# Scores of two heads at the head of every second step, and a new order of a head's products

## The reference, cut to what matters

```python
x = x + tanh(g_xattn[0]) * cross_attention(layernorm(x), ctx)        # 16 heads of 128
x = x + tanh(g_ffn[0])   * mixture_of_lora(layernorm(x))             # 2 of 8 experts of rank 16
x = x + tanh(g_xattn[1]) * sigmoid_attention(layernorm(x), ctx)
x = x + tanh(g_ffn[1])   * chosen_expert(layernorm(x))               # 1 of 8 experts of rank 64
```

## Time and profile before

| what | value |
|---|---|
| median of 3 executions | 1353.68 us (1353.68 to 1355.13) |
| the profiled execution | 1354.27 us |
| its span, first to last instruction | 1351.7 us |
| mean granted TensorE clock | 0.999 |
| TensorE matmuls busy | 1327.7 us, 98% |
| TensorE weight loads busy | 1156.7 us, 86% |
| VectorE, ScalarE busy | 766.8 and 765.9 us, 57% each |
| GpSimd busy | 65.1 us, 5% |
| DMA | 108.5 MB, 24.3% of the 16 engines' span |

### The profile page before, as it was taken

One profiled execution on the slowest core, in us unless ns is written; L12 is line 12 of the kernel. 1 busy time (PEld: TensorE's weight loads), 2 busy tenths in 40 slices (PEclk: granted clock), 3 DMA queues, 4 the chain that ended last, 5 costly groups with the idle time before them and its releaser, 6 DMA issues.

```text
span 1351.7 us, 26645 instructions
## 1 busy us (share of the span) xinstructions
PE 1327.7 (98%) x10389; PEld 1156.7 (86%) x10389; DVE 766.8 (57%) x2317; ACT 765.9 (57%) x2092; POOL 65.1 (5%) x112
## 2 busy tenths in 40 slices
PE   8899999999999999999999999999999999999998
PEld 8788888988898888988889888998889888888777
DVE  6654555646565565655656465564656555554575
ACT  4375567566465574756556564555646556456522
POOL 0000000010000000010000100001000000001010
PEclk9999999999999999999999999999999999999999
DMA  8312532123121321223212131122302112122100
GB/s 299 115 63 79 141 107 67 64 84 110 43 79 63 94 94 48 65 93 91 82 48 86 64 118 64 48 79 95 109 34 79 63 63 95 50 77 66 60 1 32
DMA packets 51451, 108.47 MB, mean 80 GB/s; under 512 B 8224, under 2 KB 32000, under 8 KB 50688
## 3 DMA queue, kind: packets, MB, share of 16 engines
q1 hardware_dynamic: 51328, 106.77, 24.3%
HBM read 89.98 MB, written 16.78 MB: 79 GB/s over the span
## 4 chain that ended last, share of the span: by engine, by line
PE 87%; DVE 9%; ACT 2%; issue 1%; DMA 0%; SPq 0%; DVEq 0%
PE bank L114 57%; PE bank L1043 8%; PE bank L1053 5%; PE bank L1014 3%; PE bank L1032 3%; PE bank L1153 2%; PE bank L1165 2%; PE bank L983 2%; PE bank L1004 1%; PE bank L1195 1%; PE bank L1107 1%; ACT xn L780 1%; DVE logit L1542 1%; DVE ao_lo L1533 1%; DVE rstd L80 1%
## 5 line engine op out<-in xcount | busy, mean ns | idle before, releaser
L114 PE MATMUL bank<-sv,ct_hi 128*128 128x256 f32 x1024 | 195.8, 290 | 0.0
L114 PE MATMUL bank<-so,ao_hi 128*128 128x256 f32 x1016 | 187.1, 283 | 0.3 <-DVE ao_lo L1533 0.3
L1533 DVE SCALAR_TENSOR_TENSOR ao_lo<-bank,vecs,ao_hi 128x512 fp32r<-128x512 f32 x127 | 95.3, 751 | 159.8 <-ACT ao_hi L749 158.9
L755 ACT ACTIVATE expo<-logit,least 128x64 f32<-128x64 f32 x512 | 171.6, 337 | 20.6 <-DVE least L1544 20.5
L749 ACT ACTIVATE ao_hi<-bank,vecs 128x512 fp32r<-128x512 f32 x127 | 87.0, 685 | 155.0 <-PE bank L1043 154.5
L114 PEld LDWEIGHTS bank<-so,ao_hi 128*128 128x128 f32 x1016 | 161.6, 188 | 8.5 <-issue 0.5
L114 PEld LDWEIGHTS bank<-sv,ct_hi 128*128 128x128 f32 x1024 | 156.7, 189 | 0.1
L1542 DVE TENSOR_TENSOR logit<-bank,rr 128x256 f32<-128x256 f32 x128 | 54.4, 425 | 162.5 <-PE bank L1053 161.9
L774 ACT ACTIVATE q_sb<-bank,qbias,qscale 128x512 f32<-128x512 f32 x128 | 99.3, 776 | 80.1 <-PE bank L114 79.6
L114 PE MATMUL bank<-sv,ct_lo 128*128 128x256 f32 x512 | 143.3, 280 | 0.0
L114 PE MATMUL bank<-so,ao_lo 128*128 128x256 f32 x508 | 141.9, 279 | 0.0
(11 more groups left out here) (239 smaller groups left out, 2666.4 us busy)
## 6 DMA issues: line engine op xcount, KB each, us to landing
sv<-v_scratch SPq DMA_DIRECT2D x56, 512.0 KB, 3.4
so<-o_scratch SPq DMA_DIRECT2D x56, 512.0 KB, 3.3
xin<-in_x_dram SPq DMA_DIRECT2D x8, 512.0 KB, 5.0
cin<-in_ctx_dram SPq DMA_DIRECT2D x32, 128.0 KB, 4.8
xres<-in_x_dram SPq DMA_DIRECT2D x8, 512.0 KB, 4.6
c_scratch<-cs SPq DMA_DIRECT2D x8, 512.0 KB, 5.0
v_scratch<-sv SPq DMA_DIRECT2D x8, 512.0 KB, 3.1
o_scratch<-so SPq DMA_DIRECT2D x8, 512.0 KB, 2.6
```

The costliest lines, as they stand in the source:

```text
L114: last = pe.matmul(out, lhs[a], rhs[b], start=start and n == 0, stop=stop and n == 2, **kw)
L755: last = act.activation(expo[:, t, :], logit[:, t, :], ACT.Exp, scale=-1.0, bias=least[:, t:t + 1], accum_out=rsum[:, t:t + 1])
L1533: dve.scalar_tensor_tensor(out=lo[:, :], in0=attention_bank(g, h)[:, :], scalar=vecs[:, v:v + 1], in1=hi[:, :].bitcast(F32), op0=ALU.add, ...
```

## The change

TensorE's step becomes: in steps of even h first scores(h-2) and scores(h-1), one behind the other; then k(h), share a, attend(h-3), share b, v(h), share c, q(h), prob_transpose(h-2), share d, output(h-3), share e. ScalarE begins a step with exps(h-2) and k's eviction; q's eviction stands ahead of its copy of the probabilities in odd steps and behind it in even ones. VectorE makes the logits of both heads at the head of an even step, waiting for the second's scores; probabilities and attn_lo come ahead of share a in even steps and behind it in odd ones; its copy of the probabilities comes behind shares b and c (before: ahead of them). The low part of the next group's context is made in step 15 of the group before. Bank 4 holds the scores of two heads; q_sb, logit, least and rsum are doubled, the exponentials overwrite the logits, and gt lies in th. Outputs lag by three heads, not four. The pipeline's emptying has a new order, and in it the last heads use banks and buffers of their own; the late weights' places move by one point. Cut to its core:

```diff
-TURN_LAG, ATT_LAG, OUT_LAG = 2, 3, 4
+TURN_LAG, ATT_LAG, OUT_LAG = 2, 3, 3
-    q_sb = sb("q_sb", [P, GT])
-    logit = sb("logit", [P, NT, SEQ])
-    expo = sb("expo", [P, NT, SEQ])
+    q_sb = sb("q_sb", [P, 2, GT])
+    logit = sb("logit", [P, 2, NT, SEQ])
-    gt = sb("gt", [E1, GT])
+    gt = th[0:E1, 0, :, :].rearrange("p c d -> p (c d)")
-    LATE_AT = {(14, "c"): 0, (14, "d"): 1, (14, "e"): 2, (15, "a"): 3, (15, "b"): 4, (15, "c"): 5, (15, "d"): 6}
+    LATE_AT = {(14, "c"): 0, (14, "d"): 1, (14, "e"): 2, (15, "b"): 3, (15, "c"): 4, (15, "d"): 5, (15, "e"): 6}
...
@@ ScalarE
         def step(b, h):
             main = live(b, h)
+            final = main and h == H - 1 and not is_body(b, NG - 1)
+            if live(b, h - TURN_LAG):
+                exps(b, h - TURN_LAG)
+            if main:
+                project(b, h, 0)
             share(b, h, "a")
             if live(b, h - ATT_LAG):
                 attn_hi(b, h - ATT_LAG)
+            share(b, h, "b")
             if main:
-                project(b, h, 0)
-            share(b, h, "b")
+                project(b, h, 1)
+                if final:
+                    split_context(b + 1)
+            share(b, h, "c")
+            soon = main and (h % 2 == 1 or (b, h) == (LAST, H - 2))
+            if soon:
+                project(b, h, 2)
             if live(b, h - TURN_LAG):
                 prob_copy(b, h - TURN_LAG)
-            share(b, h, "c")
-            if live(b, h - 1):
-                exps(b, h - 1)
-            if main:
-                project(b, h, 1)
-                if h == H - 1 and not is_body(b, NG - 1):
-                    split_context(b + 1)
+            if main and not soon:
+                project(b, h, 2)
+            if final:
+                split_tokens(b + 1)
             share(b, h, "d")
-            if main:
-                project(b, h, 2)
-                if h == H - 1 and not is_body(b, NG - 1):
-                    split_tokens(b + 1)
             share(b, h, "e")
...
@@ TensorE
         def scores(g, h):
             pe.wait_ge(pj_read.sem, pj_read.count(g, 3 * h + 2))
-            l_ready.wait(pe, g, h - 1)
+            l_ready.wait(pe, g, h - 1 if (g, h) == (LAST, H - 1) else h - 1 - h % 2)
...
         def step(b, h):
             main = live(b, h)
+            if (b, h) == (0, 2):
+                gr_read.wait(pe, 0, 2 * NT - 1)
+            if h % 2 == 0 and live(b, h - 2):
+                scores(b, h - 2)
+                scores(b, h - 1)
+            if (b, h) == (LAST, H - 1):
+                scores(b, h - 1)
+            if main and (b, h) != (0, 0):
+                project(b, h, 0)
+            share(b, h, "a")
+            if live(b, h - ATT_LAG):
+                attend(b, h - ATT_LAG)
+            share(b, h, "b")
+            if main:
+                values(b, h)
+            share(b, h, "c")
+            if (b, h) == (0, 1):
+                norms(-1)
+            if main:
+                project(b, h, 2)
+            if live(b, h - TURN_LAG):
+                prob_transpose(b, h - TURN_LAG)
+            share(b, h, "d")
             if live(b, h - OUT_LAG):
                 output(b, h - OUT_LAG)
-            if live(b, h - ATT_LAG):
-                attend(b, h - ATT_LAG)
-            share(b, h, "a")
-            if main and (b, h) != (0, 0):
-                project(b, h, 0)
-            share(b, h, "b")
-            if (b, h) == (0, 1):
-                norms(-1)
-                gr_read.wait(pe, 0, 2 * NT - 1)
-            if live(b, h - 1):
-                scores(b, h - 1)
-            if live(b, h - TURN_LAG):
-                prob_transpose(b, h - TURN_LAG)
-            share(b, h, "c")
-            if main:
-                values(b, h)
-            share(b, h, "d")
-            if main:
-                project(b, h, 2)
+            if (b, h) == (LAST, H - 1):
+                scores(b, h)
             share(b, h, "e")
...
@@ VectorE
         def step(b, h):
-            if h == 0 and not is_body(b, 0) and live(b, 0):
-                split(b, 0)
+            main = live(b, h)
+            if h % 2 == 0 and live(b, h - 2):
+                logits(b, h - 2)
+                logits(b, h - 1)
+            if (b, h) == (LAST, H - 1):
+                logits(b, h - 1)
+            if main and h == 0 and not is_body(b, 0):
+                split(b, 1)
+            if h % 2:
+                share(b, h, "a")
             if live(b, h - TURN_LAG):
                 probabilities(b, h - TURN_LAG)
-            if h == 0 and not is_body(b, 0) and live(b, 0):
-                split(b, 1)
-            share(b, h, "a")
             if live(b, h - ATT_LAG):
                 attn_lo(b, h - ATT_LAG)
-            if is_body(b, 0) and h == 1:
+            if (b, h) == (0, 1):
                 score_factors(0)
-            if live(b, h - 1):
-                logits(b, h - 1)
+            if h % 2 == 0:
+                share(b, h, "a")
+            share(b, h, "b")
+            share(b, h, "c")
             if live(b, h - TURN_LAG):
                 prob_copy(b, h - TURN_LAG)
-            share(b, h, "b")
-            share(b, h, "c")
+            if main and h == H - 1 and not is_body(b, NG - 1):
+                split(b + 1, 0)
             share(b, h, "d")
             share(b, h, "e")
...
@@ TensorE, emptying the pipeline
-        scores(LAST, H - 1)
-        gate_logits(NEXT)
-        output(LAST, H - 4)
+        turned_gates(NEXT)
+        prob_transpose(LAST, H - 2)
         attend(LAST, H - 3)
-        prob_transpose(LAST, H - 2)
+        prob_transpose(LAST, H - 1)
         attend(LAST, H - 2)
-        prob_transpose(LAST, H - 1)
         output(LAST, H - 3)
         attend(LAST, H - 1)
+        gate_logits(NEXT)
         output(LAST, H - 2)
         output(LAST, H - 1)
...
@@ VectorE, end()
             scales_at_once(LAST, 0, xres)
+            expert_scale(NEXT)
             for t in range(3):
                 chosen_expert(NEXT, t)
```

More of the change, by code:

```diff
@@ L175, in layers @@
     nqk_t = sb("nqk_t", [P, 2 * NT])
-    least = sb("least", [P, NT])
-    rsum = sb("rsum", [P, NT])
+    least = sb("least", [P, 2, NT])
+    rsum = sb("rsum", [P, 2, NT])
     rinv = sb("rinv", [P, NT])
@@ L464, in layers @@
                  "lg": (H + 1, "d"), "choice": (H + 1, "e"), "ex1": (H + 2, "a"), "scale": (H + 2, "a")}
[L465 removed]
+    LAST_CHOICE_AT = {"xn3": (14, "d"), ("xt3", 0): (15, "b"), ("xt3", 1): (15, "c")}
     def choice_at(b, h, p, name):
@@ L487, in attention_bank @@
     def attention_bank(g, h):
-        return pj_ps[0] if (g, h) == (LAST, H - 2) else pv_ps
+        return {(LAST, H - 2): pj_ps[0], (LAST, H - 1): at_ps}.get((g, h), pv_ps)
     def attention_parts(g, h):
-        return [v["k"][:, 0, 0:GT] for v in (w_hi, w_lo)] if (g, h) == (LAST, H - 2) else [ao_hi, ao_lo]
+        own = g == LAST and h >= H - 2
+        return [v["k"][:, h - (H - 2), 0:GT] for v in (w_hi, w_lo)] if own else [ao_hi, ao_lo]
     def turned_probs(g, h, t):
@@ L754, in exps @@
             for t in range(NT):
-                last = act.activation(expo[:, t, :], logit[:, t, :], ACT.Exp, scale=-1.0, bias=least[:, t:t + 1],
-                                      accum_out=rsum[:, t:t + 1])
+                last = act.activation(logit[:, h % 2, t, :], logit[:, h % 2, t, :], ACT.Exp, scale=-1.0, bias=least[:, h % 2, t:t + 1],
+                                      accum_out=rsum[:, h % 2, t:t + 1])
             last.then_inc(e_ready.sem, 1)
@@ L760, in prob_copy @@
             act.wait_ge(pt_full.sem, pt_full.count(g, h))
+            if g == LAST and h >= H - 2:
+                act.wait_ge(pv_full.sem, pv_full.count(g, h - 1))
             act.activation(pt_part(0), turned_probs(g, h, 0), ACT.Copy).then_inc(pt_ready[0].sem, 1)
@@ L773, in project @@
             else:
-                act.activation(q_sb[:, :], bank[:, :], ACT.Identity, scale=qscale[:, h:h + 1],
+                act.activation(q_sb[:, h % 2, :], bank[:, :], ACT.Identity, scale=qscale[:, h:h + 1],
                                bias=qbias[:, h:h + 1]).then_inc(pj_read.sem, 1)
@@ L949, in _ @@
             step(LAST, h)
+        exps(LAST, H - 2)
         exps(LAST, H - 1)
+        prob_copy(LAST, H - 2)
         attn_hi(LAST, H - 3)
-        prob_copy(LAST, H - 2)
+        prob_copy(LAST, H - 1)
+        attn_hi(LAST, H - 2)
+        turned_gates(NEXT)
+        attn_hi(LAST, H - 1)
         expert_exp(NEXT)
-        attn_hi(LAST, H - 2)
-        prob_copy(LAST, H - 1)
-        attn_hi(LAST, H - 1)
         end()
@@ L1027, in prob_transpose @@
                 pj_read.wait(pe, g, 3 * H - 2)
+            elif (g, h) == (LAST, H - 1):
+                l_ready.wait(pe, g, h)
             else:
-                ao_ready.wait(pe, g, h - 2 if (g, h) == (LAST, H - 1) else h - 1)
+                ao_ready.wait(pe, g, h - 1)
             bank = attention_bank(g, h)
@@ L1052, in scores @@
                     s = slice(t * P + i * SEQ, t * P + (i + 1) * SEQ)
```

(21 more changed lines are left out.)

18 lines of the change are left out of this document (11 added, 7 removed).

## The result

| | before | after |
|---|---|---|
| median | 1354.18 (4 executions) | 1338.55 (4 executions, 1337.48 to 1340.49) |
| span of the profiled execution | 1351.7 | 1334.5 |
| ScalarE busy | 765.9 | 737.5 |

The ratio is 0.9885, with a 95% interval of 0.9873 to 0.9897: 15.6 us less. The forecast was 1342 in 1331 to 1351, with 0.90 on faster. The page's costliest groups, against the earlier trace rows: the same jobs take nearly the same time each (751 ns as before; 673 against 687), but the side engines sit idle ahead of them for 77 and 29 us where it was 160 and 90, since probabilities and exponentials now stand ahead of them and fill that time.

The account below looks back on a forecast made before the run. TensorE's start-to-start times were taken to bound the kernel. Terms -15.8 + 5.1 - 2.7 - 3.1 - 1.9 - 4.0 - 0.4 + 7.2 + 0.6 + 3.5 sum to -11.5, giving about 1342 us, range 1331 to 1351.

Parts of the forecast that it names:

- Part 1: TensorE's scores of two heads run together, saving shape-change tolls of 0.25 us a pair over 63 pairs: -15.8 us.
- rival B: Scores behind scores pay the shape change again, 0.15 us in each of 63 pairs, +9.4, giving 1352; chance 0.13.
- Tolls at point b: Between attention and v, affinity and second attention enter and leave their shape alone: 0.73 us in seven groups, +5.1.
- Part 2: TensorE waits vanish: transpose -2.7 us, Gram products -3.1, late weights -1.9, start-up -4.0, end -0.4.
- start-up 4.0: First steps: less idle time and slow clock, as v is read first and scores come later; 5.3 less 1.3, -4.0 us.
- late weights 1.9: Late weights' wait for rr goes because score_factors no longer stands behind a copy: -1.9 us with its neighbours.
- The end: Emptying of the pipeline: less idle and fewer switches, but expert_scale's links stand ahead of chosen_expert; -0.4 us, bounds +1.5 and -1.6.
- Part 3: New lateness of the side engines' queues in steps 14, 15 and 6: +7.2, +0.6 and +3.5 us.
- Step 14: Groups 1 to 6: VectorE's probabilities copy, late behind variances, scales and factors, delays step 15's attention 1.2 us each, +7.2.
- Step 6: Groups 1 to 6: normalisation and tile_scales make turned_low late for mixture_rows, 0.5 us each, +3.5 with bounds 0 and 6.
- Rival A: VectorE's late places in steps 14, 15 and 6 cost near nothing instead of 11.3 us, giving 1331; chance 0.15.
- Rival C: Slower: late exponentials on ScalarE hold k's eviction, so q waits for its bank in 56 even steps, 1357; chance 0.06.

Follow-up runs that it names:

- the copy ahead: Changed kernel with score_factors moved behind VectorE's copy of the probabilities in step 14 of groups 1 to 6; 1332.84 us, ratio to before 0.9848.
- the scales early: Changed kernel with tile_scales moved from step 6 to step 2, behind VectorE's copy; 1335.25 us, ratio to before 0.9860.
- the affinity moved: Changed kernel with score_factors behind the copy and tile_scales in step 2, plus affinity's second part directly ahead of step 12's scores; 1328.40 us, ratio 0.9810.
- the matmul behind the scores: Changed kernel plus an unused full-shape 512-column matmul after the second head's scores, ahead of k's product, in 55 pairs; 1346.28 us.

## Why the prediction was right, and where it was off

**Part 1, pairs, -15.8: right, a little high.** A pair takes 0.10 + 1.08 + 0.10 = 1.28 against 1.29 in the working, with nothing between the heads, so rival B is out. Over two whole steps without side work the gain is 0.22 and not 0.25 (v of step 1 to v of step 3 of group 1: 14.95 before, 14.73 after), which makes 14 for 63 pairs; where the 0.03 between the two readings goes is not assigned. The 0.25 is the price against the order before, from its traces; against single heads ahead of k it is 0.35, which I learned only by undoing it. The new order without pairs is 0.8% slower than the kernel before, so the pairs carry more than this: they also pay for the scores' new place.

**Tolls at point b, +5.1: right.** At point b itself attention takes 0.98 ahead of the affinity instead of 0.81, and v 1.51 instead of 1.49: 0.19, as in the working. With the second attention there, 0.19 of the same kind, 0.11 in its own matmuls (1.88 against 1.77) and 0.05 in the scores make 0.35, as in the working. Sharing a toll at point d gave 0.20 (affinity) and 0.34 (second attention).

**Part 2, waits that go.** All three groups of the earlier trace rows went. Group 0 was to lose some 8.8 (eight pairs 2.0, start-up 4.0, late weights 1.9, its Gram and transpose waits 0.9) and lost 9.5. The difference is spread: up to v of step 4 it lost 4.75 where the terms give 4.5, from there to v of step 13 2.2 for 1.9, in the steps with the late weights 2.6 for 2.4. The new wait of 0.9 for k's eviction came as forecast, as did the first transpose, at 60.98. The end was sized wrong: from v of its first step to v of its last, group 7 gained 1.65, and from there to the last instruction 0.4 was lost (0.14 of it a transpose that now stands behind that v), where 0.4 was to be gained. What took it wasn't tried.

**Part 3, what is late next: places right, sizes high, and this is the miss.** The step that was mis-sized is the sum +7.2 + 0.6 + 3.5 = 11.3. By the runs it is (0.82 + 0.39) x 6 = 7.3, so 4.0 too much. On the profiled executions the gain was 17.2, 5.7 more than the 11.5 forecast: these 4.0, 0.8 in group 0, and 0.2 in each middle group. That nothing else is seen is in part luck: the pairs (by some 2) and the end (by 0.8) gained less than their terms, and side work gained what no term held.
- Step 14: "copy at 10.8 to 11.26", 1.2 each. It was at 10.54 to 10.96, mostly because three instructions of the chain start 0.08 to 0.09 before the recorded end of the one ahead (459.34, 462.21 and 464.48 in the rows of the changed kernel), which a sum of durations doesn't know. The links of the Newton steps don't: they last 0.16 and start 0.20 apart. Attention, due at 10.19, started at 11.07: 0.88 seen, 0.82 by the run.
- Step 6: turned_low, counted from the transpose of step 5, ended at 10.62, not 10.8, and mixture_rows was due at 10.49, not 10.4. 0.5 was taken, 0.36 seen, 0.39 by the run.
- The 0.1 for q in step 6 was nothing: v, transpose and q follow one another as in a step without stall.

A middle group should by the terms have given 0.3 (2.0 for pairs, 0.45 and 0.45 for the waits, less 0.7 and 1.9); it gave 1.18. 0.7 of the difference is the stalls' size. The 0.2 left are errors of opposite sign. The pairs give 0.2 less, and the transposes' wait gave 0.34, not 0.45 (0.95 from scores to transpose, 0.61 without a wait). Against that, the steps 0 to 5 gain 1.68 with the fourth block's work in them and 0.84 in group 1, which has none. 0.28 of this is the same wait, which group 1 hardly had (0.67 from scores to transpose); the other 0.55 stands in no term. It goes with the fourth block's side work, which now has other neighbours; no run tried it. Rival A (the late places cost nothing, 1331) is out, since both stalls exist and two edits took them away. Rival C didn't come about, but scales that VectorE made 1.3 later were enough to bring its mechanism about in step 15.

## What to carry to other kernels

Price a toll in the place where the work will stand, not where it stood: the same block of small products cost 0.77 ahead of a transpose and 0.82 ahead of an fp32r product. When a reordering removes a toll on the bounding engine, clock each side engine's queue over the steps with most side work, and move first whatever stands ahead of something that TensorE needs soon. Here two such moves of one line each gave 0.6%, and a third, made on a misread 0.3 us, lost 0.7% through a queue that I hadn't clocked.

## What was new about the hardware

- The change between the 64-column fp32 scores and full-width fp32r products costs 0.35 in all, out and in: 0.10 in the first full-width matmul behind, 0.10 ahead of the next scores, 0.15 in the scores themselves. The 0.10 behind is hardly the shape's: full-width fp32 attention leaves 0.09 there too.
- Between two 64-wide blocks it matters whether the form is the same. The second attention (128*64, as the scores are) beside the scores saved 0.34; the affinity (64*128) beside them only 0.20, with both blocks as long as before.
- An fp32 product's time may show in the block behind it: after norms' product (two instructions of 512 columns, 0.46 start to start) v's first matmul takes 0.52, not 0.20, and the profile shows no wait there.
- The first v product comes at one of two times, near 46.1 or near 47.3, in kernels whose start is the same: 46.1 before and 45.9 after, 47.2 with the copy ahead, 47.1 with the scales early, 46.1 with the affinity moved. The four executions with the matmul behind the scores fit this (spans 1343.3, then 1344.4 to 1344.7), though only the first has a trace. So for effects of a few tenths a group I went by the groups' times and not by spans.
